# Cross-attention and FP4 feed-forward block: joined splits, preset residuals, spread heads and a new order on VectorE and GpSimd

## The chip, the cores and the metric

The kernel runs on one core of one Trainium2 chip. The metric is device time in microseconds, 478.89 us as the median of three runs (478.62 to 481.21). TensorE (PE) multiplies matrices, VectorE (DVE), ScalarE (ACT) and GpSimd (POOL) work element by element, and the SyncE queue (SP) issues the transfers. The engines run their own instruction streams in order and wait for each other on semaphores.

## The reference

For 64 sequences of 128 rows and 256 columns: an autocorrelation attention between the normalised x and a context, then a feed-forward block whose operands are quantised to a 4-bit grid in blocks of 16.

```python
q = (Q @ Wq + bq).T; k_ = (K @ Wq + bq).T; v = (V @ Wq + bq).T
corr = real(ifft(fft(q) * conj(fft(k_)))).mean(axis=(0, 1))     # one vector of 128 lags
W_topk, I_topk = top_k(corr, 12); W_topk = softmax(W_topk)
R3 = sum(w * roll(v, -shift)); R = R3 broadcast over 16 heads, reshaped to [B, L, 256]
x = x + R @ Wout + bout
xn = layernorm(x)
def fp4_linear(x, w):        # scale = max|block| / 6, values 0 0.5 1 1.5 2 3 4 6 times scale
    return einsum('bsk,nk->bsn', fp4(x), fp4(w))
h = silu(fp4_linear(xn, w_gate)) * fp4_linear(xn, w_up)          # 704 columns
x = x + fp4_linear(h, w_down)
```

## The kernel before

There are three stretches. In the first, until about 70 us, x and the context are loaded, normalised and projected, the correlation is summed on TensorE, and the weights are quantised. The head, to about 100 us, finds the twelve best lags, multiplies the shift matrix with Wout (L867), writes the attention of all sequences to a scratch tensor in DRAM (L1119, `store_attn`), and turns the weights. Its first eight sequences get their attention through a selection matrix `pick` on TensorE (L882) and not through DRAM.

The main loop goes over 32 pairs of tiles (a tile is one sequence, 128 rows). It is a software pipeline with a step number `st`; in each step every engine works on other pairs, and the order on each engine is written out by hand. In step `st`:

- VectorE multiplies silu(gate) by up for pair st-1 (`gate_up`, L1145), takes the largest value of each block (`largest_h`, L1247), forms scales and their inverses (L1258, L1266), scales h (`scaling_h`, L1241), rounds pair st-2 to the grid (`offset_h` L945, `grid_h` L1199) and multiplies by the high part of the scale (`high_h`, L1150). For x it does the same one to two pairs ahead: `offset_x` (L945), `grid_x` (L949), `products_x` (L1150, high and low), `scaling_x` (L1234) and `largest_x` (L1271). Odd tiles also get their residual there (`residual`, L1214).
- GpSimd forms the low part of the scales (`low_scales`, L508), multiplies h by it (`low_h`, L492), adds the attention to x for pair st+5 (L548, L549; from step 1 on behind a wait for `x4_steps`, which the x grid raises) and finishes the variance (L530, L532, L534).
- ScalarE computes silu (L621), the three passes of the split of h (1408 columns) and of x (512 columns) in front of the rounding (`split`, L562, L563, L565), the normalisation (L647), the squares (L657) and the evacuation of even tiles (`residual`, L626).
- TensorE computes gate and up for two tiles (`gate_and_up`, L889 to L891) and the down projection of two older ones (`down`, L899, L901). For all tiles that are not `added` a float32 product adds x (L903).
- The SP queue transposes h (`turn_h`, L383) and x (`turn_x`, L388), stores the output (L392) and loads attention rows (`load_attn`, L370). A step's queue order is: two h transpositions, a store, the x transposition, a store, the attention loads.

In the drain (steps 31 to 35) the last pair is treated tile by tile; its h too is transposed by DMA.

## Time and profile before

| | us |
|---|---|
| median of three runs | 478.89 |
| the profiled execution's own time | 479.78 |
| its span, first to last instruction | 477.3 |
| TensorE busy | 445.2 (93%) |
| VectorE busy | 436.4 (91%) |
| ScalarE busy | 384.4 (81%) |
| GpSimd busy | 248.5 (52%) |

The mean granted TensorE clock is 0.982 of full speed. A start time in a view counts from the span's start. Instructions of an engine may overlap a little in the records, so that the spacing of their starts is what a step adds up from, not their durations.

### The profile page before, as it was taken

How to read it: one execution, taken by the hardware profiler on the slowest of the kernel's cores; microseconds unless marked ns; L12 is line 12 of the kernel's file. 1: busy time of each engine (PE TensorE's matmuls, PEld its weight loads, DVE VectorE, ACT ScalarE, POOL GpSimd, SP SyncE). 2: the span in 40 equal slices, each digit the busy share in tenths (PEclk: the TensorE clock that was granted, in tenths of full speed). 3: DMA queues.
4: the chain of work that ended last, by engine and by line, in shares of the span. 5: the costliest groups of instructions: out<-in, count | busy, mean ns of one | idle time of the engine just before them, and what ended most of it. 6: DMA issues, size and time to landing. Idle time of an engine off the chain costs nothing.

```text
span 477.3 us, 9868 instructions
## 1 busy us (share of the span) xinstructions
PE 445.2 (93%) x3362; PEld 300.8 (63%) x3362; DVE 436.4 (91%) x768; ACT 384.4 (81%) x642; POOL 248.5 (52%) x338
## 2 busy tenths in 40 slices
PE   4599995978699999999999999999999999999987
PEld 4488885844366666666666666666666666666675
DVE  3699987579999999999999999999999999999982
ACT  3369969599988888888888888888888888867572
POOL 4157750544466655665555666666666655433310
PEclk9799997999999999999999999999999999999999
DMA  7999901442256678656567666676666666555565
GB/s 242 339 349 347 345 13 33 90 90 67 59 116 138 139 121 159 128 126 129 129 130 139 140 134 139 132 134 131 139 139 137 140 116 141 107 105 106 119 139 129
DMA packets 164849, 68.66 MB, mean 144 GB/s; under 512 B 129216, under 2 KB 164544, under 8 KB 164800
## 3 DMA queue, kind: packets, MB, share of 16 engines
q1 hardware_dynamic: 164800, 68.03, 62.2%
q8 instruction: 27, 0.44, 0.4%
...
## 4 chain that ended last, share of the span: by engine, by line
PE 80%; DVE 9%; ACT 3%; DMA 3%; issue 2%; SPq 1%; POOL 1%; DVEq 0%; POOLq 0%; ACTq 0%
PE ps L889 16%; PE ps L890 15%; PE ps L891 15%; PE ps L899 15%; PE ps L901 8%; PE ps L903 3%; PE ps L740 2%; PE ps L750 2%; DMA ctx_sb<-in_ctx_dram 2%; PE ps L763 2%; DVE a_bst L994 1%; ACT h_c L565 1%; DMA hqT<-ctx_sb 1%; ACT h_c L562 1%; DVE hb L1145 1%
## 5 line engine op out<-in xcount | busy, mean ns | idle before, releaser
L889 PE MATMUL ps<-guT_hi,a_xT 128*128 128x512 f16 (+1 forms) x384 | 139.5, 363 | 7.9 <-DVE hb L1145 5.4
L890 PE MATMUL ps<-guT_lo,a_xT 128*128 128x512 f16 (+1 forms) x384 | 139.5, 363 | 0.0
L891 PE MATMUL ps<-guT_hi,a_xT 128*128 128x512 f16 (+1 forms) x384 | 139.4, 363 | 0.0
L899 PE MATMUL ps<-dT_hi,hqT 128*128 128x256 f16 x704 | 129.2, 273 | 2.6 <-DMA hqT<-ctx_sb 2.6
L901 PE MATMUL ps<-dT_lo,hqT 128*128 128x256 f16 x384 | 87.3, 273 | 0.0
L492 POOL TENSOR_TENSOR ctx_sb<-w_q_lo,sl 128x704 f16<-128x704 f16 x58 | 87.2, 1524 | 0.0
L621 ACT ACTIVATE w_raw<-ps,inv_gu 128x704 f32<-128x704 f32 x64 | 53.9, 841 | 33.4 <-PE ps L891 33.3
L899 PEld LDWEIGHTS ps<-dT_hi,hqT 128*128 128x128 f16 x704 | 68.9, 98 | 13.7 <-DMA hqT<-ctx_sb 3.7
L508 POOL TENSOR_TENSOR sl<-bm,sh 128x240 f16<-128x240 f32 (+2 forms) x34 | 20.5, 604 | 95.0 <-DVE y_h L1241 72.8
L889 PEld LDWEIGHTS ps<-guT_hi,a_xT 128*128 128x128 f16 x384 | 37.7, 98 | 45.8 <-DMA a_xT<-ctx_sb 8.6
L562 ACT ACTIVATE h_c<-y_h 128x1408 bf16<-128x1408 bf16 (+3 forms) x39 | 47.9, 1227 | 20.1 <-DVE y_h L1241 16.6
L891 PEld LDWEIGHTS ps<-guT_hi,a_xT 128*128 128x128 f16 x384 | 37.7, 98 | 38.9 <-issue 0.7
L890 PEld LDWEIGHTS ps<-guT_lo,a_xT 128*128 128x128 f16 x384 | 37.7, 98 | 37.0 <-issue 0.6
L1145 DVE SCALAR_TENSOR_TENSOR hb<-ps,h_in,w_raw 128x704 f32<-128x704 f32 x64 | 57.7, 939 | 0.8 <-ACT w_raw L621 0.6
L548 POOL TENSOR_TENSOR xs<-xs,w_raw 128x512 f32<-128x512 f32 x30 | 35.4, 1180 | 44.0 <-DVE x_c L949 44.0
L1247 DVE TENSOR_REDUCE bm<-hb 128x88 f32<-128x1408 f32 x31 | 50.2, 1620 | 1.1
L565 ACT ACTIVATE h_c<-h_c,root 128x1408 bf16<-128x1408 bf16 (+3 forms) x39 | 50.9, 1305 | 0.0
L1241 DVE TENSOR_TENSOR y_h<-hb,bm 128x1408 f32<-128x1408 f32 x31 | 50.0, 1614 | 0.0
L563 ACT ACTIVATE h_t<-y_h 128x1408 f16<-128x1408 bf16 (+3 forms) x39 | 47.3, 1212 | 0.0
L901 PEld LDWEIGHTS ps<-dT_lo,hqT 128*128 128x128 f16 x384 | 37.6, 98 | 9.2
L532 POOL TENSOR_TENSOR s_r<-s_ve,neg_half 128x2 f32<-128x2 f32 x32 | 36.3, 1136 | 2.7
L647 ACT ACTIVATE w_q_hi<-xs,s_nmr,s_r 128x256 f32<-128x256 f32 x64 | 34.9, 595 | 1.5 <-POOL s_nmr L534 1.5
...
## 6 DMA issues: line engine op xcount, KB each, us to landing
...
w_raw<-a_scratch SPq DMA_DIRECT2D x60, 128.5 KB, 2.7
hqT<-ctx_sb SPq DMA_TRANSPOSE x64, 3.8
...
```

What stands on the lines that cost most here:

```text
L492: pool.tensor_tensor(hq[:, j % 2, t, FF:2 * FF].rearrange("p (ih r) -> p ih r", ih=IH), h_g.bitcast(F16).rearrange("p (ih t r) -> p t ih r ...
L562: act.activation(c.bitcast(BF16), top, ACT.Square, scale=ANCHOR_SLOPE * unit).then_inc(done, 1)
L565: act.activation(c.bitcast(BF16), c.bitcast(BF16), ACT.Square, bias=root[:, 0:1]).then_inc(done, 1)
L621: act.activation(sil[:, i % 2, :], gu_out(i)[:, 0:FF], ACT.Silu, scale=inv_gu[:, 0:1]).then_inc(s["sil_done"], 1)
L889: pe.matmul(dst, xt[:, c, :], guT[0][:, c, n0:n1], start=(c == 0), stop=False)
L890: pe.matmul(dst, xt[:, c, :], guT[1][:, c, n0:n1], start=False, stop=False)
L891: last = pe.matmul(dst, xt[:, KC + c, :], guT[0][:, c, n0:n1], start=False, stop=(c == KC - 1))
L899: last = pe.matmul(dst, hqT[:, j % 4, c, :], dT_hi[:, c, :], start=(c == 0), stop=(added(j) and c == DCH - 1))
L901: pe.matmul(dst, hqT[:, j % 4, c, :], dT_lo[:, c, :], start=False, stop=False)
L1145: dve.scalar_tensor_tensor(out=h_v, in0=gu_out(i)[:, FF:2 * FF].rearrange(split, ih=IH), scalar=h_in[:, 0:1], in1=sil[:, i % 2, :].rearran ...
L1241: dve.tensor_tensor(y_h[:, :].rearrange(runs, ih=IH, il=2), hb[:, :].rearrange(runs, ih=IH, il=2), bm[:, 2, 0:RUN_H].unsqueeze(1).unsqueez ...
L1247: dve.tensor_reduce(bm[:, 0, 0:RUN_H], hb[:, :].rearrange("p (ih b il) -> p b ih il", ih=IH, il=2), AX.XY, ALU.max, apply_absolute_value=T ...
```

## The change

- The splits of h and x are joined: y, t and c of both lie in one row of 1920 columns (`y_hx`, `t_hx`, `c_hx`), and in steps 2 to 30 ScalarE's three split passes and VectorE's offset and grid run over all of it.
- `added` holds for every fourth tile. For the others up to tile 55, TensorE opens the output bank with one 256-column float16 product (`open_down`), ScalarE overwrites the bank with x times `out_fac` (`preset_x`), and `down` adds to that. Tiles 56 to 61 take the float32 product ahead of their wait.
- VectorE's order in a step is new: scales, residual, inverses, h scaling, offset, grid, x products, x scaling, high product, largest x. The attention sum of GpSimd (`attend`) stands ahead of the variance and no longer waits for `x4_steps`.
- The values of the first eight sequences are spread over the heads by GpSimd (`v_head`), and TensorE multiplies them directly (`attend_head`); the selection matrix goes. The warming products before the main loop are cut and moved (`filler`).
- In the drain, tiles 62 and 63 are transposed on TensorE in parts, evacuated by ScalarE and VectorE, and their residual is VectorE's (`last_residual`); tiles 60 and 61 get products tile by tile. ScalarE's last h split stands ahead of the silu of tile 63.

VectorE, a steady step, before (scale, offset, grid and products of h and x):

```order
L1247 TENSOR_REDUCE bm<-hb 128x88 [waits h_steps]
L945 TENSOR_TENSOR h_t<-h_c,h_t 128x1408 [waits h_split]
L1258 SCALAR_TENSOR_TENSOR bm<-bm,tiny 128x120 [waits sh_done,sl,x_max,h_steps]
L1199 TENSOR_TENSOR w_q_lo<-h_c,h_t 128x1408 [waits loh,h4_steps]
L945 TENSOR_TENSOR x_t<-x_c,x_t 128x512 [waits x_split]
L1150 TENSOR_TENSOR ctx_sb<-w_q_lo,sh 128x8x2x88 [waits hT3,hT2,h4_steps]
L949 TENSOR_TENSOR x_c<-x_c,x_t 128x512 [waits x4_steps]
L1214 SCALAR_TENSOR_TENSOR a_xT<-ps,inv_out,xs 128x256 [waits stored3,d_done]
L1266 RECIPROCAL bm<-bm 128x120 [waits sc_steps]
L1150 TENSOR_TENSOR ctx_sb<-x_c,sh 128x8x2x32 [waits sl,xT0,x4_steps]
L1150 TENSOR_TENSOR ctx_sb<-x_c,sl 128x8x2x32
L1241 TENSOR_TENSOR y_h<-hb,bm 128x1408 [waits h_split,sc_steps]
```

VectorE, the corresponding step after, one that has a residual:

```order
L1413 TENSOR_REDUCE bm<-hb 128x88 [waits h_steps]
L1424 SCALAR_TENSOR_TENSOR bm<-bm,tiny 128x120 [waits sh_done,sl,x_max,h_steps]
L1377 SCALAR_TENSOR_TENSOR a_xT<-ps,inv_out,xs 128x256 [waits stored1,d_done]
L1432 RECIPROCAL bm<-bm 128x120 [waits sc_steps]
L1407 TENSOR_TENSOR y_hx<-hb,bm 128x1408 [waits h_split,sc_steps]
L1074 TENSOR_TENSOR t_hx<-c_hx,t_hx 128x1920 [waits h_split]
L1344 TENSOR_TENSOR w_q_lo<-c_hx,t_hx 128x1920 [waits loh,h4_steps]
L1291 TENSOR_TENSOR ctx_sb<-w_q_lo,sh 128x8x2x32 [waits sl,xT1,h4_steps]
L1291 TENSOR_TENSOR ctx_sb<-w_q_lo,sl 128x8x2x32
L1400 TENSOR_TENSOR y_hx<-w_q_hi,bm 128x512 [waits h_split]
L1291 TENSOR_TENSOR ctx_sb<-w_q_lo,sh 128x8x2x88 [waits hT1,hT0,h4_steps]
```

The residual and the inverses follow the scales, the h scaling comes ahead of offset and grid, these have 1920 columns, and the x products lie behind the grid; the h product with `sh` is now behind the x scaling.

GpSimd, a steady step, before (L508 low scales, L492 low products, L548 the attention sum):

```order
L508 TENSOR_TENSOR sl<-bm,sh 128x240 [waits sh_done,sl,x4_steps,sc_steps,loh,yx_done,yh_done]
L492 TENSOR_TENSOR ctx_sb<-w_q_lo,sl 128x704 [waits hT0,hT1,sl,h4_steps]
L492 TENSOR_TENSOR ctx_sb<-w_q_lo,sl 128x704
L530 TENSOR_SCALAR s_ve<-s_sq 128x2 [waits xn_ready,sq_done]
L532 TENSOR_TENSOR s_r<-s_ve,neg_half 128x2 [waits pool_st]
L534 TENSOR_TENSOR s_nmr<-s_nm,s_r 128x2 [waits pool_st]
L548 TENSOR_TENSOR xs<-xs,w_raw 128x512 [waits pool_st,x4_steps,attn_loaded0]
L549 TENSOR_TENSOR s_nm<-neg_mean,w_raw 128x2
```

GpSimd, the corresponding step after (L547, L531, L560):

```order
L547 TENSOR_TENSOR sl<-bm,sh 128x240 [waits sh_done,sl,x4_steps,sc_steps,loh,yx_done,yh_done]
L531 TENSOR_TENSOR ctx_sb<-w_q_lo,sl 128x704 [waits hT2,hT3,sl,h4_steps]
L531 TENSOR_TENSOR ctx_sb<-w_q_lo,sl 128x704
L560 TENSOR_TENSOR xs<-xs,w_raw 128x512 [waits pool_st,attn_loaded1]
L561 TENSOR_TENSOR s_nm<-neg_mean,w_raw 128x2
L584 TENSOR_SCALAR s_ve<-s_sq 128x2 [waits xn_ready,sq_done]
L586 TENSOR_TENSOR s_r<-s_ve,neg_half 128x2 [waits pool_st]
L588 TENSOR_TENSOR s_nmr<-s_nm,s_r 128x2 [waits pool_st]
```

The attention sum with its small second part moved ahead of the three variance instructions, and has lost its wait for `x4_steps`.

The diff, cut to its core:

```diff
-K_H, K_HQ, K_XQ, K_W, K_R = 3, 3, 4, 4, 3
+K_H, K_HQ, K_XQ, K_W, K_R = 3, 3, 2, 4, 3
...
 FIRST, END = -4, NP + 4
-A_BANK = (4, 6, 0, 1)
-PICK_BANK = (2, 3, 5, 7)
+A_BANK = (6, 0, 1, 2)
+HEAD_BANK = (3, 4, 5, 7)
+GU_BANK = (0, 1, 2, 3, 6, 0, 1, 2)
 N_PIECES = 4
+CUT = FF // P
+PARTS = ((0, CUT), (CUT, DCH), (CUT, CUT + 3), (CUT + 3, DCH))
+TURNS = ((0, 0), (0, 1), (1, 0), (1, 2), (1, 3))
...
         def added(i):
-            return i % 2 == 1 and i // 2 < NP - 4
+            return i % 4 == 1 and i // 2 < NP - 4
+
+        def preset(i):
+            return i >= 2 and i % 4 != 1 and i // 2 < NP - 4
...
+        def joined(st):
+            return pair_ok(st - 2) and pair_ok(st + 1)
...
+                if i // 2 == NP - 2:
+                    sp.wait_ge(s["z_lo"], 2 + i % 2)
...
-            pool.wait_ge(s["w_split"], 3 * N_GU)
-            pool.memset(pick[:, :, :], 0.0).then_inc(s["pick_set"], 1)
...
+            pool.wait_ge(s["late_loaded"], 32)
+            pool.wait_ge(s["trx"], 2)
+            pool.tensor_tensor(xs[:, 0:4, :], xs[:, 0:4, :], bout_bc[:, 0:D].unsqueeze(1).broadcast_to([P, 4, D]), ALU.add)
+            pool.wait_ge(s["trc"], 2 * NQ)
+            pool.wait_ge(s["v_ev"], 2)
+            for two in range(2):
+                last = pool.tensor_copy(
+                    v_head[:, two].rearrange("p t (h r) -> p t h r", r=ROWS8),
+                    v_all[:, 0:4 * DH].rearrange("p (t r two) -> p t r two", t=4, two=2)[:, :, :, two].unsqueeze(2).broadcast_to(
+                        [P, 4, HEADS, ROWS8]))
+            last.then_inc(s["spread_v"], 1)
...
+            def attend(n):
+                if pair_ok(n) and n >= 2:
+                    pool.wait_ge(attn_loaded[n % 2], 32 * (n // 2))
+                    if n == 2:
+                        pool.wait_ge(s["x1_done"], 2)
+                    if n <= 5:
+                        need(pool, s["yx_done"], n - 2)
+                    need(pool, s["pool_st"], K_R * (n - 3))
+                    x1 = xs[:, 2 * n:2 * n + 2, :]
+                    pool.tensor_tensor(x1, x1, attn[:, n % 2, :, 0:D], ALU.add)
+                    pool.tensor_tensor(s_nm[:, n % 4], neg_mean[:, 2 * n:2 * n + 2], attn[:, n % 2, :, D], ALU.add
+                                       ).then_inc(s["x1_done"], 1)
...
+                if st >= 1:
+                    attend(st + 5)
...
+                        x_gridded(act, n - 1)
+                    split(x_t, x_c, y_x, s["x_split"], 3 * n, X_SCALE)
 
             def split_h(j):
                 act.wait_ge(s["yh_done"], j + 1)
-                need(act, s["h4_steps"], K_HQ * (j - 1) + 2)
-                split(h_t[:, :], h_c[:, :], y_h[:, :], s["h_split"], 3 * j, X_SCALE)
+                if joined(j + 2):
+                    act.wait_ge(s["yx_done"], j + 4)
+                if j >= 1:
+                    act.wait_ge(s["h4_steps"], K_HQ * (j - 1) + 2)
+                else:
+                    x_gridded(act, 2)
+                both = slice(0, 2 * FF + (2 * D if joined(j + 2) else 0))
+                split(t_hx[:, both], c_hx[:, both], y_hx[:, both], s["h_split"], 3 * j, X_SCALE)
+
+            def preset_x(i):
...
                     square_x(st + 4)
                     scale_high(st)
+                    residuals(2 * st - 7)
                     silu(2 * st)
+                    preset_x(2 * st - 6)
+                    if st == 1:
+                        evacuate_weights(act, range(GU_FILLS + 2, GU_FILLS + 3))
+                    if st == 2:
+                        evacuate_weights(act, range(GU_FILLS + 4, len(FILLS)))
+                    normalise_x(st + 3)
+                    if st == NP - 1:
+                        split_h(j)
+                    silu(2 * st + 1)
+                    preset_x(2 * st - 5)
+                    if st < NP - 1:
+                        split_h(j)
                     if st == 1:
                         evacuate_weights(act, range(GU_FILLS + 3, GU_FILLS + 4))
-                    normalise_x(st + 3)
...
             pe.wait_ge(s["w_hi"], N_GU)
             pe.wait_ge(s["evx"], 2 * NQ)
             pe.wait_ge(s["evc"], 2 * NQ)
+            def filler(n):
+                pe.wait_ge(s["v_ev"], 2)
+                for _ in range(n):
...
 
-            pe.wait_ge(s["v_ev"], 2)
-            for _ in range(8):
-                pe.matmul(bank(6)[:, 0:P], ones[:, :], ident[:, :], start=True, stop=True)
...
+
+            def attend_head(j):
                 for h in range(2):
-                    if g == 0:
-                        pe.wait_ge(s["t_steps"], 10 + h)
+                    if j == 0:
+                        pe.wait_ge(s["t_steps"], 9 + h)
+                    last = pe.matmul(bank(HEAD_BANK[j])[:, 0:DA], v_head[:, h, j, :], wp[:, h, :], start=(h == 0), stop=(h == 1))
+                last.then_inc(s["direct"], 1)
+
+            def attend(g):
+                pe.wait_ge(s["w_ev"], EARLY + g + 1)
+                for h in range(2):
                     last = pe.matmul(bank(A_BANK[g])[:, 0:DA], v_rows[:, P * g:P * (g + 1), h], wp[:, h, :],
                                      start=(h == 0), stop=(h == 1))
                 last.then_inc(s["t_pe"], 1)
-                if g == 1:
-                    pe.wait_ge(s["t_steps"], 12)
-                    pe.wait_ge(s["pick_set"], 2)
-                    for j in range(4):
-                        pe.matmul(bank(PICK_BANK[j])[:, 0:DA], pick[:, j, :], a_sb[:, 0, :], start=True, stop=True).then_inc(s["picked"], 1)
+
+            pe.wait_ge(s["spread_v"], 1)
+            pe.wait_ge(s["w_ev"], EARLY)
+            attend_head(0)
+            attend_head(1)
+            attend(0)
+            attend_head(2)
+            attend_head(3)
+            for g in range(1, 4):
+                attend(g)
...
 
             def down(j):
-                dst = bank(6 + j % 2)[:, 0:D]
-                pe.wait_ge(hT[j % 4], 16 * (j // 4 + 1))
-                out_ready(pe, j - 2)
+                final = j // 2 == NP - 1
+                late = j >= 2 * (NP - 4) and not final
+                dst = bank(2 * (1 - j % 2) if final else 6 + j % 2)[:, 0:D]
+                if final:
+                    if j % 2 == 0:
+                        turn_last(0)
+                elif preset(j):
+                    pe.wait_ge(s["o_set"], n_preset(j))
+                else:
+                    out_ready(pe, j - 2)
+                if late:
+                    pe.matmul(dst, ident_out[:, :], xs[:, j, :], start=True, stop=False)
+                if not final:
...
+                            pe.wait_ge(s["z_ev_v"], 1)
+                        else:
+                            pe.wait_ge(s["z_ev"], 4 if c else 3)
...
                 last.then_inc(s["d_done"], 1)
 
-            pe.wait_ge(s["t_steps"], 15)
+            def turn_last(t):
+                for k in range(len(TURNS)):
+                    if TURNS[k][0] == t:
+                        dst = turned(k)[0]
+                        c0, c1 = PARTS[TURNS[k][1]]
+                        pe.wait_ge(s["z_done"], 2 * t + (1 if c0 == 0 else 2))
+                        for c in range(c0, c1):
+                            last = pe.transpose(dst[:, c - c0, :], hq[:, (NP - 1) % 2, t, c * P:(c + 1) * P], ident16[:, :])
+                        last.then_inc(s["z_turn"], 1)
+
+            pe.wait_ge(s["t_steps"], 14)
             pe.wait_ge(s["w_ev"], GU_FILLS)
             pe.wait_ge(s["x1_done"], 2)
             pe.wait_ge(s["w_lo"], len(SEGS))
             for f in range(GU_FILLS, GU_FILLS + 2):
                 transpose_weights(f)
-            pe.wait_ge(s["id_out"], 1)
-            for _ in range(28):
+            for _ in range(20):
                 pe.matmul(bank(4)[:, 0:P], ones[:, :], ident[:, :], start=True, stop=True)
             def gate_and_up(i):
                 pe.wait_ge(xT[(i // 2) % 2], 16 * (i // 4 + 1))
                 need(pe, s["h_steps"], K_H * ((i - 2) // 2) + 1 + i % 2 if i >= 2 else 0)
                 gu_bank(i, 0)
                 gu_bank(i, 1).then_inc(s["gate_done"], 1)
+                if i >= 8:
...
+
+            def open_down(j):
+                if tile_ok(j) and preset(j):
+                    out_ready(pe, j - 2)
+                    pe.matmul(bank(6 + j % 2)[:, 0:D], ident16[:, :], dT_hi[:, 0, :], start=True, stop=False).then_inc(s["o_open"], 1)
 
...
-
-            dve.tensor_scalar(inv_out[:, :], w_inv[:, 1:2], h_tmp[:, 1:2], None, ALU.mult).then_inc(cs, 1)
-            dve.wait_ge(cs, 5)
-            dve.reciprocal(out_fac[:, :], inv_out[:, :]).then_inc(cs, 1)
+
+            add_head(0)
+            keep_attn(0)
+            add_head(1)
+            for g in range(1, 4):
+                keep_attn(g)
...
+                dve.wait_ge(s["d_done"], i + 1)
+                dve.wait_ge(stored[i % 4], 16 * (i // 4))
+                dve.scalar_tensor_tensor(out=of[:, i % 4, :], in0=bank(2 * (1 - t))[:, 0:D], scalar=inv_out[:, 0:1], in1=xs[:, i, :],
+                                         op0=ALU.mult, op1=ALU.add).then_inc(s["o_last"], 1)
+
             def residual(i):
...
                 if pair_ok(j) and st < NP:
                     gate_up(2 * j)
+                    if st == 1:
+                        largest_x(3)
                     gate_up(2 * j + 1)
                     largest_h(j)
                 if st < NP:
+                    scales(st)
+                    if tile_ok(2 * st - 7) and added(2 * st - 7):
+                        residual(2 * st - 7)
+                    inverses(st)
+                    if scaled(st):
+                        dve.wait_ge(sc, 2 * (st - SC0) + 2)
+                    if pair_ok(j) and st < NP - 1:
+                        scaling_h(j)
                     if pair_ok(p):
                         offset_h(p)
-                    scales(st)
-                    if pair_ok(p):
                         grid_h(p)
-                    if st >= 1 and pair_ok(xa):
+                    elif st >= 1:
                         offset_x(xa)
-                    if pair_ok(p) and st < NP - 1:
-                        high_h(p)
-                    if st >= 1 and pair_ok(xa):
                         grid_x(xa)
-                    if pair_ok(st - 4):
-                        residual(2 * st - 7)
-                    inverses(st)
                     if st >= 1 and pair_ok(xa):
                         products_x(xa)
-                    if scaled(st):
-                        dve.wait_ge(sc, 2 * (st - SC0) + 2)
-                    if pair_ok(j):
+                    if st == NP - 1:
                         scaling_h(j)
-                    if st == NP - 1:
                         high_h(p)
                         low_h(p)
                     if pair_ok(xb):
                         scaling_x(xb)
-                    if st >= 0:
+                    if pair_ok(p) and st < NP - 1:
+                        high_h(p)
+                    if st >= 1:
                         largest_x(st + 3)
                 if st == NP:
                     gate_up(2 * j)
                     last_y(0)
                     offset_h(p)
                     grid_h(p)
-                    high_h(p)
-                    low_h(p)
+                    for t in range(2):
+                        turned_products(p, t)
                     gate_up(2 * j + 1)
                     last_scale(1)
                     last_y(1)
                     last_grid(0)
                     last_grid(1)
+                    dve.wait_ge(s["z_turn"], 4)
+                    dve.wait_ge(s["d_done"], 2 * NP - 4)
+                    src, dst = turned(3)
+                    dve.tensor_copy(dst, src).then_inc(s["z_ev_v"], 1)
+                    last_residual(0)
+                    last_residual(1)
 
 
```

## Rows read from the trace of the kernel before

**Rows 1.** Busy time by stretch: length, then each engine, PEclk, DMA share, GB/s
```profile
200.00:300.00 100.00, 100.00 (x643) 63.68 (x641) 99.69 (x142) 87.18 (x142) 61.02 (x71) 1.00 0.63 136
```

**Rows 2.** VectorE in order of time, one step: start, us, instruction
```profile
284.52 0.68 DVE L1234 TENSOR_TENSOR w_raw<-w_q_hi,bm 128x512 f32<-128x512 f32 x1
...
287.55 1.62 DVE L1247 TENSOR_REDUCE bm<-hb 128x88 f32<-128x1408 f32 x1
...
289.88 0.28 DVE L1258 SCALAR_TENSOR_TENSOR bm<-bm,tiny 128x120 f32<-128x120 f32 x1
...
291.21 0.89 DVE L1150 TENSOR_TENSOR ctx_sb<-w_q_lo,sh 128x1408 f16<-128x1408 f16 x1
292.02 0.42 DVE L949 TENSOR_TENSOR x_c<-x_c,x_t 128x512 f16<-128x512 bf16 x1
292.35 0.48 DVE L1214 SCALAR_TENSOR_TENSOR a_xT<-ps,inv_out,xs 128x256 f32<-128x256 f32 x1
292.75 0.90 DVE L1266 RECIPROCAL bm<-bm 128x120 f32<-128x120 f32 x1
293.55 0.48 DVE L1150 TENSOR_TENSOR ctx_sb<-x_c,sh 128x512 f16<-128x512 f16 x1
...
295.83 0.68 DVE L1234 TENSOR_TENSOR w_raw<-w_q_hi,bm 128x512 f32<-128x512 f32 x1
```

**Rows 3.** VectorE in the drain, dependent neighbours
```profile
457.14 0.89 DVE L945 TENSOR_TENSOR h_t<-h_c,h_t 128x1408 f16<-128x1408 bf16 x1 [1.68 <-ACT h_c L565]
458.06 0.89 DVE L1199 TENSOR_TENSOR w_q_lo<-h_c,h_t 128x1408 f16<-128x1408 bf16 x1
```

**Rows 4.** TensorE, the float32 residual product of one tile, then the next tile
```profile
251.99 0.60 PE L903 MATMUL ps<-xs,ident_out 128*128 128x256 f32 x2
252.42 0.27 PE L899 MATMUL ps<-dT_hi,hqT 128*128 128x256 f16 x1
```

**Rows 5.** GpSimd in the same step
```profile
285.33 0.64 POOL L508 TENSOR_TENSOR sl<-bm,sh 128x240 f16<-128x240 f32 x1 [2.55 <-DVE y_h L1241]
285.93 3.00 POOL L492 TENSOR_TENSOR ctx_sb<-w_q_lo,sl 128x704 f16<-128x704 f16 x2
```

**Rows 6.** VectorE beside GpSimd, and once without it
```profile
103.80 0.69 DVE L1234 TENSOR_TENSOR w_raw<-w_q_hi,bm 128x512 f32<-128x512 f32 x1
...
112.33 0.86 DVE L1150 TENSOR_TENSOR ctx_sb<-x_c,sh 128x512 f16<-128x512 f16 x1
...
428.96 0.37 DVE L1150 TENSOR_TENSOR ctx_sb<-x_c,sh 128x512 f16<-128x512 f16 x1
```

**Rows 7.** GpSimd in the first steps
```profile
103.92 0.62 POOL L534 TENSOR_TENSOR s_nmr<-s_nm,s_r 128x2 f32<-128x2 f32 x1
...
110.08 0.19 POOL L534 TENSOR_TENSOR s_nmr<-s_nm,s_r 128x2 f32<-128x2 f32 x1
111.73 1.18 POOL L548 TENSOR_TENSOR xs<-xs,w_raw 128x512 f32<-128x512 f32 x1 [1.46 <-DVE x_c L949]
```

**Rows 8.** Queue SPq in the same step; the page's line on landing
```profile
283.09 1.26 SPq L388 DMA_TRANSPOSE a_xT<-ctx_sb  x1
...
285.02 1.20 SPq L370 DMA_DIRECT2D w_raw<-a_scratch  x2
...
w_raw<-a_scratch SPq DMA_DIRECT2D x60, 128.5 KB, 2.7
```

**Rows 9.** Head: queue, landing of its load, TensorE
```profile
79.63 0.33 SPq L361 DMA_DIRECT2D cT<-w_scratch  x1
...
cT<-w_scratch SPq DMA_DIRECT2D x1, 64.0 KB, 1.8
...
82.94 1.03 PE L867 MATMUL ps<-wout_sb,cT 128*128 128x257 f32 x4
```

**Rows 10.** Drain: VectorE's last product, ScalarE's last evacuation
```profile
468.00 0.52 DVE L1186 TENSOR_TENSOR ctx_sb<-w_q_lo,sl 128x704 f16<-128x704 f16 x1
...
474.64 0.48 ACT L626 ACTIVATE a_xT<-ps,inv_out 128x256 f32<-128x256 f32 x1 [1.81 <-PE ps L903]
```

270 lines of the change are left out of this document (160 added, 110 removed).

## The prediction

> **What bounds the kernel now.** I read the page first, then the busy times by stretch, then VectorE (DVE) in order of time over one step, then GpSimd (POOL) and the queues over the same step. Between 200 and 300 us TensorE is busy for 100.00 us and VectorE for 99.69, ScalarE for 87.18 and GpSimd for 61.02 [rows 1]. By these busy times alone one would say that only TensorE's work counts. VectorE in order of time says something else: nine rows of one step, from one x scaling (L1234) to the next, show no idle time, each instruction starting 0.1 us or less before the record of the last one ends, and the step is 11.31 us [rows 2]. So two engines are full at the same time. A change that frees TensorE alone is worth nothing; the step will be what VectorE needs. I therefore count VectorE first.
>
> **The VectorE step, part by part.** Gone: the separate x offset and x grid, each 0.33 (the grid from 292.02 to 292.35) [rows 2]; and, in every second step, the residual L1214, 292.35 to 292.75 = 0.40, so 0.20 a step. Together -0.86. Added: offset and grid now run over 1920 columns in place of 1408. A 1408-column pass of two-byte data takes 0.89, one of 512 columns 0.42 [rows 2], so 512 more columns cost 512 x 0.47/896 = 0.27, twice 0.27 = +0.54. The first x product loses its meeting with GpSimd's small addition (0.48 at 293.55 [rows 2], 0.37 at 428.96 where GpSimd no longer adds [rows 6]): -0.11.
>
> The new order has a price of its own. Before, an instruction that needs the result of the one in front of it had another between them nearly everywhere. Where two such stand side by side in the drain, 457.14 to 458.06, the second starts 0.92 after the first, which is longer than its 0.89 [rows 3]; with an independent one behind it, the same length gives 291.21 to 292.02 = 0.81 [rows 2]. A dependent neighbour thus costs 0.11 to 0.12. The new order puts side by side: largest value and scales, scales and inverses (in the half of the steps without a residual), inverses and the h scaling, offset and grid, grid and x products: 4.5 x 0.12 = +0.54. The sum is -0.86 + 0.54 - 0.11 + 0.54 = +0.11 a step, 11.4 us. From step 2 to step 30 that is 29 x 0.1 = +3 us. The sum is little, but it is not the gain that fewer instructions suggest.
>
> By the Trainium skill ("VectorE: DVE Perf Modes", The DRAIN you can't avoid) a semaphore between two chained VectorE instructions costs nothing extra. By that rule the +0.54 goes, which is a rival below; the trace does not agree, with 0.92 against 0.81.
>
> **The port between VectorE and GpSimd.** At 103.80 VectorE began a scaling of two SBUF operands that took 0.69 [rows 6]; GpSimd's two-element product began at 103.92 and took 0.62, until 104.54, where it takes 0.19 alone [rows 7]. The other way round, GpSimd's addition of attention to x began at 111.73 and took 1.18 [rows 7], and VectorE's product from 112.33 took 0.86 instead of 0.37 [rows 6]: it ended 0.28 behind that addition. So one waits while the other reads. In the old steady step the large addition was held back by a wait for x4_steps, and then lay beside a residual and a reciprocal, which have at most one SBUF operand; it cost only the 0.11 above.
>
> The change removes that wait and puts the addition right behind the two low products. I lay the new step out from the start of the x scaling L1234 (0.00). VectorE: high product at 0.60, x maximum 1.41, gate-and-up products 2.0, largest value at 3.84 (3.03 of [rows 2] plus 0.81), scales at 3.84 + 1.65 = 5.49. GpSimd: its low scales are triggered at 0.81 (285.33 - 284.52), meet the high product that has begun, and end near 1.9; the low products, 3.00 for two, end near 4.9 [rows 5]. The addition needs the attention rows. Their loads stand on the SP queue behind the x transposition, which waits for the x products; these now end beside the x scaling, where before they stood in front of the h scaling. From the transposition at 283.09 to the first load at 285.02 are 1.93, the second begins 0.6 later, and a load lands 2.7 after its issue [rows 8]. So they land at 0.1 + 1.93 + 0.6 + 2.7 = 5.3 to 5.4, and the addition starts within 0.1 us of the scales at 5.49, which read two SBUF operands.
>
> If VectorE is first, it loses nothing there, but GpSimd's small operations then meet the h scaling, offset and grid. If GpSimd is first, the scales wait for about 1.1 of its 1.18. Bounds for the port are thus 0 and 1.06 a step, in the 24 steps that have both (3 to 26). I take 0.3, nearer to the case in which VectorE is first, since that is what its 5.49 against a landing of 5.3 plus a hand-over allows and no row decides: 24 x 0.3 = +7.
>
> By the Trainium skill ("SBUF — State Buffer", Who interferes with whom) a VectorE instruction with two SBUF inputs and a GpSimd instruction that reads SBUF exclude each other for the whole instruction, whoever issues first. The rows above agree, 0.86 against 0.37 and 0.62 against 0.19.
>
> **TensorE and ScalarE.** In every four tiles two float32 residual products (251.99 to 252.42 = 0.43 each [rows 4]) become three opening products of 256 columns at about 0.11: 0.86 - 0.33 = 0.53, 0.27 a step. TensorE needs 11.0, under VectorE's 11.4, so this is hidden. ScalarE gains three starts by joining and pays 1.5 presets and half a residual more; it has some 13% idle [rows 1], so I price that at nothing. If its cover were gone it would cost up to 0.5 a step.
>
> **Head.** The correlation weights load issued at 79.63 with 1.8 to landing is there at 81.4, yet the product with it starts at 82.94, behind eight warming products [rows 9]. These move ahead, one VectorE copy of 0.3 goes, but the spread heads add four TensorE products in front of the last attention groups, and VectorE keeps these groups before the first x maximum. I take -1.2; bounds -2 and +1 (the second if the granted clock is at its lower level there).
>
> **Drain.** VectorE waits 1.68 at 457.14 for ScalarE's split, which stood behind a silu [rows 3]; the split now goes first. From the last product's end, 468.00 + 0.52, to the span's end at 477.3 are 8.8, through two DMA transpositions and two output tiles, the last evacuation at 474.64 [rows 10]. On TensorE the last transpositions, an evacuation, six or seven products, an addition and a store of 2.2 come to about 5.0. The sum of both, -5.5, is the upper bound. The tiles 60 and 61 still come by DMA and TensorE takes all four in order behind them, so I take -4.3; the other bound is -2.
>
> **Sum.** +3 + 7 - 1.2 - 4.3 = +4.5 on the profiled execution's own 479.8 (span 477.3 and 2.5 around it): 484.3. The runs' median lies 0.9 below the profiled one, so 483.4. A measurement of this kernel tells about 0.5%, 2.4 us, from no change.
>
> **Rivals.**
> - The port costs nothing: the addition falls between two VectorE instructions with one SBUF operand each. For it: its landing is an estimate to 0.1 us. Against: the window in which it must fall is smaller than the addition. Then +3 - 5.5 = -2.5: 476.4, give or take 4. Chance 0.32.
> - GpSimd is first in every step: the scales wait 1.06, 24 x 1.06 = 25 in place of 7: 501. Place: scales behind attend's addition; it decides as soon as the loads land before 5.4. Chance 0.12.
> - The addition comes second, but the three small operations of the variance behind it each wait for a long VectorE instruction (the h scaling, offset, grid), the normalisation of x on ScalarE comes late, and the split behind it ends after VectorE wants to scale h again. That is some 1.3 in every second step, 24 x 0.65 = 16: 492. Chance 0.16.
> - Side-by-side instructions cost nothing: VectorE needs 11.31 + 0.11 - 0.54 = 10.9, TensorE's 11.0 decides, 29 x -0.3 = -9 and -5.5: 465. Against it stands 0.92 at equal length. Chance 0.06. (This is the way the time would go by the rule of the Trainium skill in The DRAIN you can't avoid.)
> - The forecast, 483.4, with its own range 478 to 489: chance 0.34.
>
> **Range and chances.** From 472 to 499: this leaves out the fourth rival and over half of the second, 0.13 in all. Faster by over 0.5%: three quarters of the first rival, the fourth, and a little of the forecast (0.04), 0.34. Within 0.5%: the rest of the first rival and the lower end of the forecast, 0.15. Slower: 0.51.
>
> **What would show it.** The spacing of the x scaling in steps 5 to 25: 11.4 without port waits, 11.7 as forecast, over 12.2 if GpSimd is first. The scales (120 elements, 0.28 now) would be recorded with 0.3 to 1.3. TensorE would show idle time of some tenths in each step, before the opening product or the first gate product, and the chain of waits would name VectorE for most of the span. The drain from the last VectorE product to the end would be 5 to 6 instead of 8.8, and the first gate product would start near 99 instead of 100.3. I am wrong if VectorE shows idle time in the steady step, since then another engine sets it, or if dependent neighbours start as closely as others.

## The result, and the profile after

The changed kernel takes 495.81 us (median of four runs, 494.44 to 497.41) where the kernel before takes 479.20: a ratio of 1.033, 95% interval 1.030 to 1.036. It is 16.6 us slower. The forecast was 483.4, slower by 4.5. The profiled execution of the changed kernel is the slowest of its four (497.41), so that the spans below are 18.3 apart and not 16.6.

| | before | after |
|---|---|---|
| span of the profiled execution | 477.3 | 495.6 |
| first gate product | 100.32 | 99.68 |
| x scaling of step 1 | 114.98 | 115.84 |
| x scaling of step 29 | 431.10 | 451.24 |
| from there to the end | 46.2 | 44.4 |

Of the 18.3 us between the two spans, +0.9 lie ahead of the x scaling of step 1, +19.3 between it and that of step 29, and -1.8 behind. The x scalings, 11.30 apart before, are now between 10.76 and 12.63 apart: 12.04 in the mean of the 25 with an attention addition between them, and 11.43 (before 11.18) in the last three, which have none.

The busy times of the stretch that [rows 1] shows of before (length, then each engine, PEclk, DMA share, GB/s):

```profile
200.00:300.00 100.00, 92.99 (x603) 57.86 (x601) 97.25 (x114) 83.04 (x122) 72.39 (x67) 1.00 0.62 127
```

TensorE lost 7 of 100 us and VectorE now has 2.75 of idle time. GpSimd, with the same work, is recorded as busy for 72.39 instead of 61.02: it waits inside its instructions. VectorE in order of time, one step (this answers to [rows 2]; columns are start, us, instruction):

```profile
235.18 0.68 DVE L1400 TENSOR_TENSOR y_hx<-w_q_hi,bm 128x512 f32<-128x512 f32 x1
235.79 0.88 DVE L1291 TENSOR_TENSOR ctx_sb<-w_q_lo,sh 128x1408 f16<-128x1408 f16 x1
236.59 0.67 DVE L1437 TENSOR_REDUCE bm<-w_q_hi 128x32 f32<-128x512 f32 x1
237.19 1.79 DVE L1286 SCALAR_TENSOR_TENSOR hb<-ps,h_in,w_raw 128x704 f32<-128x704 f32 x2
239.01 1.62 DVE L1413 TENSOR_REDUCE bm<-hb 128x88 f32<-128x1408 f32 x1
240.67 1.11 DVE L1424 SCALAR_TENSOR_TENSOR bm<-bm,tiny 128x120 f32<-128x120 f32 x1
241.71 0.47 DVE L1377 SCALAR_TENSOR_TENSOR a_xT<-ps,inv_out,xs 128x256 f32<-128x256 f32 x1
242.10 0.89 DVE L1432 RECIPROCAL bm<-bm 128x120 f32<-128x120 f32 x1
243.02 1.63 DVE L1407 TENSOR_TENSOR y_hx<-hb,bm 128x1408 f32<-128x1408 f32 x1
```

GpSimd in the same step and in the next (this answers to [rows 5, 7]):

```profile
240.47 1.18 POOL L560 TENSOR_TENSOR xs<-xs,w_raw 128x512 f32<-128x512 f32 x1 [0.34 <-DMA w_raw<-a_scratch]
241.60 0.24 POOL L561 TENSOR_TENSOR s_nm<-neg_mean,w_raw 128x2 f32<-128x2 f32 x1
...
253.44 1.18 POOL L560 TENSOR_TENSOR xs<-xs,w_raw 128x512 f32<-128x512 f32 x1 [0.87 <-DMA w_raw<-a_scratch]
254.58 1.58 POOL L561 TENSOR_TENSOR s_nm<-neg_mean,w_raw 128x2 f32<-128x2 f32 x1
256.24 0.98 POOL L584 TENSOR_SCALAR s_ve<-s_sq 128x2 f32<-128x2 f32 x1
257.31 1.62 POOL L586 TENSOR_TENSOR s_r<-s_ve,neg_half 128x2 f32<-128x2 f32 x1
259.01 0.20 POOL L588 TENSOR_TENSOR s_nmr<-s_nm,s_r 128x2 f32<-128x2 f32 x1
```

Read the two together. At 240.47 the addition starts 0.2 ahead of the scales, due at 240.67, and a 0.28 instruction is recorded with 1.11. At 253.44 VectorE was first: its scales (253.11) cost nothing, and the h scaling, which begins at 254.36 as the addition ends, is recorded with 1.74 in place of 1.62. But each of GpSimd's two-element instructions then waits for a long one of VectorE's, so that `s_nmr`, which needs 0.2, comes at 259.01. ScalarE, in order, waits for it, here and again one step on (in brackets the idle time ahead and who ended it):

```profile
259.25 1.09 ACT L697 ACTIVATE w_q_hi<-xs,s_nmr,s_r 128x256 f32<-128x256 f32 x2 [2.48 <-POOL s_nmr L588]
...
271.69 1.09 ACT L697 ACTIVATE w_q_hi<-xs,s_nmr,s_r 128x256 f32<-128x256 f32 x2 [2.71 <-POOL s_nmr L588]
272.69 0.83 ACT L665 ACTIVATE w_raw<-ps,inv_gu 128x704 f32<-128x704 f32 x1
273.42 0.46 ACT L743 ACTIVATE ps<-xs,out_fac 128x256 f32<-128x256 f32 x1
273.81 1.79 ACT L604 ACTIVATE c_hx<-y_hx 128x1920 bf16<-128x1920 bf16 x1
```

The joined split starts 2.3 behind the x scaling of 271.52 in place of 0.8, and VectorE's h scaling, which writes what the split reads, waits for its end:

```profile
277.32 0.90 DVE L1432 RECIPROCAL bm<-bm 128x120 f32<-128x120 f32 x1
279.19 1.62 DVE L1407 TENSOR_TENSOR y_hx<-hb,bm 128x1408 f32<-128x1408 f32 x1 [0.97 <-ACT c_hx L607]
```

Between 140 and 400 us ScalarE waited 31 us for `s_nmr`, 12 times; before, its longer waits there were for TensorE and VectorE only. Little of the 31 us reaches VectorE, which between these times sat idle for 2.4 us behind ScalarE (1.6 ahead of the h scaling, 0.8 ahead of the largest x). ScalarE's wait:

```profile
ACT w_q_hi L697 <- POOL s_nmr L588: 31.1, 12, 4.0
```

There is a third case. In 23 of the 25 steps with an addition GpSimd waits for its attention rows (`<-DMA w_raw`), and these do not come at one time: the addition starts between 4.9 and 7.2 after the x scaling. Where it starts at 6.2 or later, in 6 steps, it meets the h scaling or the offset behind it, which read two SBUF tensors each. GpSimd and VectorE, in one such step:

```profile
350.60 1.18 POOL L560 TENSOR_TENSOR xs<-xs,w_raw 128x512 f32<-128x512 f32 x1 [1.68 <-DMA w_raw<-a_scratch]
...
350.71 2.55 DVE L1407 TENSOR_TENSOR y_hx<-hb,bm 128x1408 f32<-128x1408 f32 x1
```

The 19.3 us between the x scalings of steps 1 and 29 can be added up from the records of VectorE:

| | us | steps |
|---|---|---|
| VectorE's own new order (the undisturbed steps of 11.34 and 11.61 against 11.30 and 11.18) | 4.3 | 28 |
| scales recorded with over 0.28 | 7.5 | 10 |
| h scaling or offset recorded with over 1.62 or 1.15 | 4.8 | 7 |
| VectorE idle behind ScalarE | 2.7 | 7 |

### The profile page after: what moved, and what is told of

It is laid out like the page before. It is cut to its first block, busy times and chain, and to the rows that moved or that the text cites. A ratio compares the mean times of both kernels' runs of the same rounds, so it can differ in the third digit from the quotient of the medians.

```text
span 495.6 us, 9781 instructions
## 1 busy us (share of the span) xinstructions
PE 445.3 (90%) x3383; PEld 294.8 (59%) x3383; DVE 450.0 (91%) x700; ACT 393.3 (79%) x612; POOL 292.3 (59%) x340
## 4 chain that ended last, share of the span: by engine, by line
PE 34%; DVE 18%; POOL 16%; issue 13%; ACT 13%; DMA 4%; SPq 1%; POOLq 0%; ACTq 0%; DVEq 0%
PE ps L980 6%; PE ps L981 6%; PE ps L982 6%; POOL ctx_sb L531 5%; ACT c_hx L604 4%; PE ps L1010 4%; ACT c_hx L607 4%; POOL xs L560 3%; POOL s_r L586 3%; POOL s_nm L561 3%; PE ps L1013 2%; DVE hb L1286 2%; PE ps L834 2%; DVE bm L1413 2%; DVE y_hx L1400 2%
## 5 line engine op out<-in xcount | busy, mean ns | idle before, releaser
L1010 PE MATMUL ps<-dT_hi,hqT 128*128 128x256 f16 x704 | 125.3, 273 | 2.1 <-ACT ps L743 1.6
L547 POOL TENSOR_TENSOR sl<-bm,sh 128x240 f16<-128x240 f32 (+2 forms) x34 | 36.8, 1084 | 92.1 <-DVE y_hx L1400 85.9
L531 POOL TENSOR_TENSOR ctx_sb<-w_q_lo,sl 128x704 f16<-128x704 f16 x58 | 87.1, 1521 | 2.7 <-DVE ctx_sb L1291 2.7
L604 ACT ACTIVATE c_hx<-y_hx 128x1920 bf16<-128x1920 bf16 (+4 forms) x42 | 61.9, 1474 | 17.4 <-DVE y_hx L1400 8.7
L607 ACT ACTIVATE c_hx<-c_hx,root 128x1920 bf16<-128x1920 bf16 (+4 forms) x42 | 65.4, 1556 | 0.0
L605 ACT ACTIVATE t_hx<-y_hx 128x1920 f16<-128x1920 bf16 (+4 forms) x42 | 61.5, 1464 | 0.0
L1407 DVE TENSOR_TENSOR y_hx<-hb,bm 128x1408 f32<-128x1408 f32 x31 | 53.2, 1716 | 3.0 <-ACT c_hx L607 2.1
L560 POOL TENSOR_TENSOR xs<-xs,w_raw 128x512 f32<-128x512 f32 x30 | 38.3, 1276 | 26.2 <-DMA w_raw<-a_scratch 26.2
L1074 DVE TENSOR_TENSOR t_hx<-c_hx,t_hx 128x1920 f16<-128x1920 bf16 (+4 forms) x42 | 41.7, 993 | 3.7 <-ACT c_hx L607 3.7
```

The costliest lines, as they stand in the source:

```text
L531: pool.tensor_tensor(hq[:, j % 2, t, FF:2 * FF].rearrange("p (ih r) -> p ih r", ih=IH), h_g.bitcast(F16).rearrange("p (ih t r) -> p t ih r ...
L604: act.activation(c.bitcast(BF16), top, ACT.Square, scale=ANCHOR_SLOPE * unit).then_inc(done, 1)
L605: act.activation(t.bitcast(F16), top, ACT.Copy, scale=STICKY * unit).then_inc(done, 1)
L607: act.activation(c.bitcast(BF16), c.bitcast(BF16), ACT.Square, bias=root[:, 0:1]).then_inc(done, 1)
L1010: last = pe.matmul(dst, hqT[:, j % 4, c, :], dT_hi[:, c, :], start=(c == 0 and not late and not preset(j)), stop=(c == DCH - 1 and j > 0))
```

## The experiments

Times are medians, ratios are to the kernel before on the same chip, with 95% intervals. The two last columns are the mean distance of x scalings, of the 25 with an addition between them and of the last three.

| run | us | ratio | with addition | without |
|---|---|---|---|---|
| after | 495.8 | 1.033 (1.030 to 1.036) | 12.04 | 11.43 |
| e1 two columns | 483.3 | 1.008 (1.005 to 1.010) | 11.50 | 11.43 |
| e2 one operand | 497.1 | 1.037 (1.033 to 1.041) | 12.12 | 11.43 |
| e3 variance first | 492.7 | 1.027 (1.024 to 1.030) | 11.89 | 11.43 |
| e4 by turns | 487.6 | 1.016 (1.013 to 1.020) | 11.78 | 11.32 |
| e5 old orders | 476.0 | 0.991 (0.989 to 0.994) | 11.30 | 10.92 |
| e6 turns, variance | 490.2 | 1.021 (1.018 to 1.023) | 11.80 | 11.32 |
| e7 no presets | 495.9 | 1.033 (1.028 to 1.037) | 12.02 | 11.61 |
| e8 odd added | 477.0 | 0.994 (0.992 to 0.997) | 11.30 | 11.18 |
| e9 more fillers | 475.0 | 0.989 (0.986 to 0.992) | 11.30 | 10.92 |
| e10 window | 480.4 | 1.001 (0.999 to 1.003) | 11.43 | 11.11 |
| e11 split first (in before) | 479.6 | 1.000 (0.999 to 1.002) | 11.30 | 11.18 |
| e12 early addition | 489.4 | 1.020 (1.016 to 1.024) | 11.82 | 10.92 |

**e1, the addition made small.**

```diff
-pool.tensor_tensor(x1, x1, attn[:, n % 2, :, 0:D], ALU.add)
+pool.tensor_tensor(x1[:, :, 0:2], x1[:, :, 0:2], attn[:, n % 2, :, 0:2], ALU.add)
```

> The changed kernel, in which GpSimd adds only 2 of every 256 attention columns to x from tile 4 on (the rest of the attention is left out); order, waits and semaphores stay. Theory (the port and what follows from GpSimd's lateness): the steps of 12.17 go to the 11.53 that steps 27 to 30 have without the addition, 24 x 0.63 = 15: about 481, and the scales L1424 take 0.28 in every step. Rival (VectorE's own work in the new order and the joined splits set the step): the time stays within 3 us of 495.8.

Measured 483.3, 12.5 less than the change, with steps of 11.34 without a residual and 11.61 with one in turn (in five of the 25 more, up to 12.47, most of them behind a late `s_nmr`). The scales by lines and shapes, 140 to 400 us, of this kernel and then of the changed one (busy us, mean ns | idle before):

```profile
L1424 DVE SCALAR_TENSOR_TENSOR bm<-bm,tiny 128x120 f32<-128x120 f32 x23 | 6.6, 287 | 0.8
```

```profile
L1407 DVE TENSOR_TENSOR y_hx<-hb,bm 128x1408 f32<-128x1408 f32 x21 | 37.0, 1760 | 2.2 <-ACT c_hx L607 1.6
...
L1074 DVE TENSOR_TENSOR t_hx<-c_hx,t_hx 128x1920 f16<-128x1920 bf16 x21 | 26.1, 1242 | 0.0
...
L1424 DVE SCALAR_TENSOR_TENSOR bm<-bm,tiny 128x120 f32<-128x120 f32 x22 | 13.2, 602 | 0.8
```

So 12.5 of the 16.6 us come from this one GpSimd instruction and what follows from it: 0.32 a step in the scales, and 0.13 and 0.09 in h scaling and offset (1760 and 1242 ns against 1626 and 1151 in this run); idle time differs by under 0.1 a step. What is left against before is nearly all VectorE's own order: 11.50 against 11.30. (The 11.53 of the expectation was a mean over four distances, one of them with an addition.)

**e2, scales with one SBUF tensor.**

```diff
-dve.scalar_tensor_tensor(out=bm[:, 1, n0:n1], in0=bm[:, 0, n0:n1], scalar=SIXTH * X_SCALE, in1=tiny[:, n0:n1], ...)
+dve.tensor_scalar(bm[:, 1, n0:n1], bm[:, 0, n0:n1], SIXTH * X_SCALE, tiny[:, 0:1], ALU.mult, ALU.max)
```

> The changed kernel with VectorE's scales reading one SBUF tensor instead of two (the floor comes as one column per partition). Theory (a VectorE instruction waits for GpSimd only when it reads two SBUF tensors): the scales never take 0.7 to 1.3 again, the addition runs under scales, residual and inverses, 0.33 a step goes, 24 x 0.33 = 8: about 488; the h scaling is still hit in some steps. Rival (the wait is not tied to the number of operands): 495.8 within 2.

My theory failed. The scales read one tensor, and still wait, 721 ns in the mean, with single ones at 1.29:

```profile
L1424 DVE TENSOR_SCALAR bm<-bm,tiny 128x120 f32<-128x120 f32 x22 | 15.9, 721 | 0.8
```

Counting SBUF tensors is thus not enough to tell what waits for GpSimd. The Trainium skill ("SBUF — State Buffer", Who interferes with whom) says that a `tensor_scalar` on SBUF data can run in a mode that takes both read ports and then contends too. The 721 ns agree with that. The runs don't show which mode it was in: at 0.28 it was no faster than the other form.

**e3, variance ahead of the addition.**

```diff
-                if st >= 1:
-                    attend(st + 5)
                 n = st + (4 if st < 0 else 3)
...
-                if st < 1:
-                    attend(st + 5)
+                attend(st + 5)
```

> The changed kernel with GpSimd's three variance instructions put back ahead of the attention addition, still without the wait for the x grid. Theory of the port: the addition then starts at about 6.1 after the x scaling and the h scaling, due at 6.7, waits about 0.7 in every step: 11.5 + 0.7 = 12.2, about 496, with ScalarE no longer waiting for s_nmr. Rival (the late variance and the late normalisation are what costs): 10 us less, about 486.

492.7, between the two. ScalarE no longer waits for `s_nmr` at all, and the wait sits in one place, the h scaling, in all but one of the steps from 2 to 25 (there the offset has it):

```profile
L1404 DVE TENSOR_TENSOR y_hx<-hb,bm 128x1408 f32<-128x1408 f32 x22 | 45.0, 2044 | 0.8
```

2044 against 1626 ns are 0.42 a step, not 0.7: the addition, started at 227.32, ended at 228.50 beside the reciprocal and the first 0.7 of the h scaling (due at 227.81); in a step with a residual the h scaling is due 0.27 later and waits for less. The net gain is 3 us. It fits the 2.7 us that VectorE sat idle behind ScalarE in the change, but the edit also moved the addition from one VectorE instruction to another, so that the late normalisation alone is not shown to cost 3. The port by itself is the larger part.

**e4, offset and grid by turns.**

```diff
-offset(c_hx[:, part_of(p)], t_hx[:, part_of(p)]).then_inc(h4, 1)
+offset(x_c, x_t).then_inc(h4, 1)
+offset(h_c, h_t).then_inc(h4, 1)
```

and the grid in the same way, with waits only for the instruction two places ahead.

> The changed kernel with offset and grid done apart again, by turns: x offset, h offset, x grid, h grid, then the x products, so that none of them needs the one in front of it; ScalarE's joined passes stay. Theory (a dependent neighbour costs 0.12): 0.34 + 0.80 + 0.34 + 0.80 = 2.27 in place of 1.185 + 1.19 = 2.375 a step, -3 us, 492.8. Rival (neighbours cost nothing, only starts and columns count): two more starts, +0.13 a step, +4 us, 499.6.

Without an addition the distance is 11.32 where it is 11.43 in the change, e1, e2 and e3, 0.11 less, though two more instructions start in each: the cost of dependent neighbours is shown, at the size forecast. The time fell by 8.2, not 3. The rows show where the rest is: with little or no harm to VectorE the addition can start only between 5.5 after the x scaling, behind the scales, and about 5.9; later it reaches into the h scaling. It did so in 11 steps here and in 8 of the change. It starts when its attention rows land; why they land when they do, no run settles.

**e5, the orders of before.** The x split apart, VectorE's, ScalarE's and GpSimd's orders as before; presets, opening products, head and drain as changed.

```diff
+                    else:
+                        pool.wait_ge(s["x_grid"], 2 * (n - 3))
...
+                    if pair_ok(p):
+                        offset_h(p)
                     scales(st)
+                    if pair_ok(p):
+                        grid_h(p)
+                    if st >= 1 and pair_ok(xa):
+                        offset_x(xa)
...
```

> The changed kernel with VectorE's, ScalarE's and GpSimd's step orders and the separate x split of the kernel before; presets, opening products, spread heads and the new drain stay. Theory (the loss is in the joined splits and the new orders, head and drain are worth 2 to 3): below the kernel before, 473 to 478; a step of VectorE 11.1 with a residual every second step, but in the steps without it the attention addition outlasts the reciprocal and the x products wait some 0.4. Rival (the presets on ScalarE cost, too): above 480.

476.0, below the kernel before by 0.9%. Of the 4.5 us between the two profiled spans, 1.8 lie ahead of the x scaling of step 1, 0.9 in the steps and 1.8 in the drain. The steps tell where the gain ends. Without an addition they are 10.79 and 11.18 apart; with it every one is 11.30, although half of them have no residual. In those the addition is longer than the reciprocal beside it, and the x product waits 0.4:

```profile
245.28 0.89 DVE L1429 RECIPROCAL bm<-bm 128x120 f32<-128x120 f32 x1
245.50 1.18 POOL L562 TENSOR_TENSOR xs<-xs,w_raw 128x512 f32<-128x512 f32 x1 [1.55 <-issue]
...
246.10 0.86 DVE L1291 TENSOR_TENSOR ctx_sb<-w_q_lo,sh 128x512 f16<-128x512 f16 x1
```

**e6, by turns and variance first together.**

> The changed kernel with both edits that helped: offset and grid by turns for x and h, and the variance ahead of the attention addition. If the two costs are apart, their gains add: 495.8 - 8.2 - 3.1 = 484.5, a step of about 11.6 to 11.7. Rival (both take away the same wait, the late split of ScalarE): 487 to 488.

490.2, worse than e4 alone. Its steps are 11.77 nearly everywhere, which is e3's 11.88 less the 0.11 of the turns, where e4's went from 11.22 to 12.49. The gains do not add: with the variance first the addition cannot start before 6.2 after the x scaling and always meets the h scaling or the offset, and e4's short steps are gone. Neither forecast named that.

**e7, no presets.**

```diff
-            return i % 4 == 1 and i // 2 < NP - 4
+            return i % 2 == 1 and i // 2 < NP - 4
```

with the float32 products for the other tiles up to 55.

> The changed kernel with the output residuals as before: a float32 product for every even tile, VectorE for every odd one; no opening products and no presets. Theory (VectorE sets the step and its window of one-operand work behind the scales gets 0.4 longer in every second step): +0.2 a step of own work, less port wait, in sum within 4 of 495.8. Rival (the presets make ScalarE late): 5 or more below, under 491.

495.9, no change. In sum presets and opening products neither cost nor gain in the new order. In the steps without an addition the half residual that they spare VectorE does show, 11.43 against 11.61 here; with one the distances are the same, 12.04 and 12.02, as the theory had it: a longer stretch behind the scales is hit less.

**e8, old orders, every odd residual on VectorE.**

> The kernel of the run with the old orders, but every odd tile's residual on VectorE and presets for the even tiles alone. Theory (VectorE is full, its order is that of before): steps of 11.30 as before, gains only from head and drain: 476 to 477, and the x products are not hit by the attention addition. Rival (TensorE set the step with VectorE): steps of 11.2 or less, 474.

477.0, and 11.30 in every step, with the x product at 475 ns or less. Against e5 a residual of 0.40 in every second step is exchanged for a wait of 0.4. The steps stay exactly the same, so in e5 the moved residual is worth nothing while there are additions.

**e9, more warming products (e5 with 32 for 20).**

> The kernel of the run with the old orders, with 32 warming products in place of 20 ahead of the first gate product. With 20 TensorE had 3.0 us of idle time there, and in five of nine profiles (the changed kernel's among them) the granted clock then fell to half for some 3 us and the first step took 12.7 in place of 11.2. Theory (the idle time lets the clock fall): idle time of about 1.8, no half clock, the runs end at the lower end of the 474.6 to 476.7 of that kernel: 474.6. Rival (the clock there has nothing to do with it): 476.

475.0 us. TensorE's idle time ahead of the first gate product went to 0.3, not 1.8, and the clock stayed up. Busy times of this kernel, then of the changed one, and of before (the column ahead of the last two is PEclk):

```profile
98.00:100.00 2.00, 1.69 (x15) 1.27 (x14) 0.28 (x1) 1.68 (x4) 1.88 (x4) 1.00 0.52 97
100.00:102.00 2.00, 2.00 (x11) 0.94 (x10) 1.82 (x5) 2.00 (x7) 0.00 (x0) 1.00 0.45 87
```

```profile
100.00:102.00 2.00, 2.00 (x9) 0.81 (x8) 1.70 (x5) 2.00 (x7) 0.00 (x0) 0.73 0.28 78
102.00:104.00 2.00, 2.00 (x7) 0.73 (x6) 1.77 (x4) 0.32 (x3) 1.59 (x4) 0.50 0.62 143
```

```profile
102.00:104.00 2.00, 2.00 (x13) 1.08 (x11) 1.90 (x6) 2.00 (x6) 0.97 (x3) 1.00 0.48 147
```

But e5's own profile had 3.0 of idle time at full clock, as had e1, e2, e3 and e12, where in the changed kernel, e4, e6, e7, e8 and e10 the clock fell to half behind the same 3.0 to 3.2. So this idle time alone does not decide it. The interval of e5 overlaps with this one's, too, so that the 1.0 us between them is not shown to be the clock's.

**e10, a wider window (e5 with the largest x value moved).**

```diff
                     inverses(st)
+                    if st >= 1:
+                        largest_x(st + 3)
...
-                    if st >= 1:
-                        largest_x(st + 3)
```

and `normalise_x` ahead of the silu on ScalarE.

> The kernel of the run with the old orders, with the largest value of x moved from behind the x scaling to behind the inverses, and ScalarE's normalisation moved ahead of the silu of the even tile. Theory (a step is full with what VectorE and GpSimd must read apart from each other): the window beside the attention addition grows by 0.6 and the x product no longer waits 0.4 in every second step, but the low h products then reach past the end of VectorE's one-operand stretch and the h offset waits about as much: 11.25 to 11.30 a step, 475 to 476. Rival (only the window at the addition counts): 11.02 a step as without the addition, 24 x 0.28 = 7 less, 469.

480.4, steps of 11.31 and 11.51 in turn. The x product waits no more. The h offset does, 1018 ns in place of 882, as the low products now end behind its due start:

```profile
L1410 DVE TENSOR_REDUCE bm<-hb 128x88 f32<-128x1408 f32 x23 | 37.3, 1620 | 0.8
L1074 DVE TENSOR_TENSOR t_hx<-c_hx,t_hx 128x1408 f16<-128x1408 bf16 x23 | 23.4, 1018 | 2.2
```

The rival (469) is out, and the theory's 475 to 476 was short by 5. The last steps tell why: the two behind the last addition are 11.31 and 11.50 apart, as all the others, so that the addition now costs nothing and the step is set elsewhere. The h offset starts 0.19 later than in e5, counted from the largest value (404.61 in one of these steps), when ScalarE's split of h has just ended (404.58): with the largest x gone from in front of it VectorE comes to it sooner than ScalarE. Another 0.13 go beside the low products, the part of this that the port can explain. In steps without a residual the largest x begins another 0.14 late, as ScalarE's normalisation ends (408.93) just ahead of it (408.96). In the steps this makes 3.8 us over e5; 1.6 more lie ahead of the x scaling of step 1.

**e11, the split first, in the kernel before.**

```diff
+                    if st == NP - 1:
+                        split_h(j)
                     silu(2 * st + 1)
-                    split_h(j)
+                    if st < NP - 1:
+                        split_h(j)
```

> The kernel before, with one swap: in the last step of the loop ScalarE's split of h stands ahead of the silu of the last tile. VectorE's wait of 1.68 at 457.14 goes. Theory (in the drain TensorE has eight tiles of 2.3 to multiply and VectorE's lateness shows only in its idle 1.95 and 0.68): up to 1.7 less, 477.2 to 478. Rival (TensorE's backlog hides it): no change, 478.9.

479.6, no change. VectorE's last product ended at 466.96 instead of 468.52, yet the span is 477.1. The rival's number was right and its reason is not what this trace shows: the transposition of the last tile took 4.87 here, where the one of before, issued at 468.5, took 3.5, and TensorE waited for it. The chains of waits of this kernel and of the one before follow; the second shows the tile in front of the last, whose transposition is the one that TensorE waited for there. What made the last one longer, and whether it was so in all twelve executions, is not shown:

```profile
466.99 4.87 DMA hqT<-ctx_sb
471.90 0.28 PE ps L902
```

```profile
466.30 3.50 DMA hqT<-ctx_sb
469.85 0.28 PE ps L899
```

**e12, the addition's place alone (e5 with it as in the change).**

```diff
-                    else:
-                        pool.wait_ge(s["x_grid"], 2 * (n - 3))
...
+                if st >= 1:
+                    attend(st + 5)
                 n = st + (4 if st < 0 else 3)
...
-                attend(st + 5)
+                if st < 1:
+                    attend(st + 5)
```

> The kernel of the run with the old orders, with GpSimd's attention addition alone put as the change puts it: ahead of the variance and with no wait for the x grid. Theory (the addition must lie beside one-operand work of VectorE, and the wait held it there): it starts when the low products end, 4.4 after the x scaling, just ahead of the h offset, which then waits about 1.05; without the addition a step is 11.02, so 12.05 in place of 11.30, 24 x 0.75 = 18 more than 476: 494. Rival (the loss of the change came from its joined splits and VectorE's order, the addition's place matters only with them): 475 to 478.

489.4, 13.4 over e5. In 20 of the 24 steps from 2 on the h offset, 882 ns in e5, is recorded with 1.74 us; in the other four the rows landed later, and the scales or the x offset waited. The mean of the h offset:

```profile
L1075 DVE TENSOR_TENSOR t_hx<-c_hx,t_hx 128x1408 f16<-128x1408 bf16 x22 | 34.9, 1584 | 0.0
```

So moving one GpSimd instruction and dropping its wait costs two thirds of the 19.8 us between e5 and the change, in the old order as well; the joined splits and the orders of VectorE and ScalarE account for the 6.4 that are left. Place and wait went together, so which of the two it is was not separated. It is less than the 18 forecast, as the offset is stretched by 0.86, not 1.05.

## Why the prediction was right and wrong

**The side and the place were right.** VectorE was taken as the bound, the drop of instructions as worth little, and the port as the largest term; so they came. The steps' own cost was put at +0.1 a step, +3 us; e1 gives +0.2 (11.50 against 11.30), and the undisturbed steps add up to +4.3. The 0.12 for a dependent neighbour holds: the largest value takes 1.65 from start to start where it took 1.54, and e4 takes 0.11 out. The count missed that the first x product, priced like the one at 428.96 of before, takes 0.34 from start to start in the new order (450.57 to 450.91) and 0.28 there (428.96 to 429.24).

**The step that failed is the port's term: "If VectorE is first, it loses nothing there", and with it "I take 0.3", +7 us.** The port and what follows from it cost 15.0 us, 0.6 in each of the 25 steps. The bounds, 0 and 1.06, held, and the scales alone came to just the 0.3 a step: 10 of 25 took 0.7 to 1.3, in sum 7.5 us. That this equals the 7 is in part luck, as a mean over hit and missed steps. What was put at nothing is the other half.

First, the landing of the attention rows was worked out once, at 5.3 to 5.4, and taken for all steps. Of the 23 steps in which it waited for its rows, the addition started at 5.3 to 5.5 in 8 and later in 14, up to 7.2. In 7 of these the h scaling or the offset waits for the addition, which no term and no rival had: 4.8 us.

Second, where VectorE is first, the addition and the four small instructions behind it meet h scaling, offset and grid; the late variance makes ScalarE late, and the joined split hands that to the h scaling of the next step. That was a rival with a chance of its own (492, 0.16), priced at 16 us as if it excluded the other cases. In the trace the cases share the steps, often a late one in front of an early one, and all are paid; but this one comes to 2.7 us only. In sum it is 19.3 us in 28 steps against the 10 forecast for 29.

e1 takes the addition away, e3 moves it behind the variance, e12 moves it in the old order, and the time moves by -12.5, -3.1 and +13.4: that the port between the two engines is what costs is shown by these. The three-way split of the 15.0 us is read from one trace.

**The head** was to give 1.2 and cost 0.9. The first gate product came 0.6 earlier, but behind 3.0 us without work, and the clock fell to 0.50 between 102 and 104; that was named as the bound +1. In e2, whose head is the same and whose clock stayed up, the x scaling of step 1 comes at 113.95, 1.0 earlier than before, but in e3, also at full clock, at 115.26. A single profile does not tell this term to better than 1 us.

**The drain** was to give 4.3 and gave 1.8. From the last VectorE product, 487.56, to the end are 8.0, not 5 to 6. The working added up VectorE's tail and forgot what was already queued on TensorE: eight tiles of 2.3. The busy times from the last gate product to the last down product, after and then before:

```profile
473.50:493.00 19.50, 18.96 (x170) 15.98 (x169) 14.16 (x27) 11.90 (x21) 0.88 (x2) 1.00 0.52 119
```

```profile
453.30:474.60 21.30, 18.67 (x153) 15.24 (x150) 12.92 (x21) 11.62 (x18) 1.53 (x2) 1.00 0.67 145
```

Before, 2.6 us were idle there, and only these could be had; 18.96 of 19.50 are now work.

**Of the signs named ahead,** the scales at 0.3 to 1.3 and the idle TensorE came as told; "I am wrong if VectorE shows idle time" came, too: 2.75 of 100 us. Of these, 1.3 are waits for ScalarE; the rest are gaps of a few hundredths in front of instructions that need their neighbour.
